# A convolutional recurrence on quarter arrays: the vertical pass of the second layer, with its transfers in pieces tied to its steps

## The reference, cut to what matters

```python
def _L1_conv_ref(x, down_w, down_b, right_w, right_b, left_w, left_b):
    def _conv1d(x, w, b):              # 5 taps, 48 channels to 48
        y = jax.lax.conv_general_dilated(x, w, window_strides=(1,), padding=[(2, 2)], ...)
        return y + b[None, :, None]
    def step(w, b):
        def f(carry, inp):
            nxt = inp + _conv1d(carry, w, b)
            return (nxt, nxt)
        return f
    xs = jnp.moveaxis(x, 2, 0)         # rows of the image
    _, d_rest = jax.lax.scan(step(down_w, down_b), d0, xs[1:])     # down
    _, u_rest = jax.lax.scan(step(down_w, down_b), u0, seq)        # and up again
    ...                                # then the same over columns, right and left
```

## Time and profile before

| | |
|---|---|
| median of 3 runs | 12709.53 us (12704.08 to 12710.47) |
| the profiled execution, its own time | 12698.42 us |
| its span | 12696.6 us |
| mean granted clock of TensorE | 0.985 |
| vertical stage, first to last matmul record | 2447.9 to 3774.7 us |
| horizontal stage, first to last matmul record | 3821.4 to 5151.8 us |

### The profile page before, as it was taken

The page is one execution under the profiler, slowest core; times in us unless marked ns, Lnnn a source line. Parts: engine busy times, 40 slices in busy tenths (PEclk is TensorE's granted clock), DMA queues, the critical chain, the costliest instruction groups (busy, mean ns, idle before and its releaser), DMA issues. The chain is left out here.

```text
span 12696.6 us, 315986 instructions
## 1 busy us (share of the span) xinstructions
PE 12256.2 (97%) x126170; PEld 8471.7 (67%) x126170; DVE 7918.9 (62%) x17482; ACT 5425.8 (43%) x11157; POOL 4647.4 (37%) x3557
## 2 busy tenths in 40 slices
PE   7999999899989999899999999999998999999999
PEld 6877434477767777555555555555556888888887
DVE  0000577533334544588888888888886777777777
ACT  0000111211213333455555555555555777777776
POOL 0000222100000045566666666666663444434444
PEclk9999999999999999899999999999999999999999
DMA  4333456783765488666666666666662222222222
GB/s 128 133 132 131 130 154 158 162 156 67 154 124 157 139 211 227 103 88 89 88 88 89 88 88 88 89 88 88 89 86 68 54 56 55 54 54 56 55 56 53
DMA packets 2310008, 1323.93 MB, mean 104 GB/s; under 512 B 1872228, under 2 KB 2219867, under 8 KB 2222959
## 3 DMA queue, kind: packets, MB, share of 16 engines
q1 hardware_dynamic: 2041484, 1201.47, 47.6%
q10 hardware_dynamic: 267232, 104.65, 3.5%
HBM read 648.72 MB, written 450.74 MB: 87 GB/s over the span
## 5 line engine op out<-in xcount | busy, mean ns | idle before, releaser
L1583 PE MATMUL l_m<-l_wa,l_pix 128*128 128x288 f32 x8192 | 2211.2, 413 | 14.0 <-DMA l_left<-k_rim_dram 14.0
L1583 PEld LDWEIGHTS l_m<-l_wa,l_pix 128*128 128x128 f32 x8192 | 1475.3, 190 | 699.9 <-issue 376.5
L1439 POOL TENSOR_TENSOR l_qkv<-l_qkv,l_copies 128x576 f32<-128x576 f32 x1024 | 1437.2, 1403 | 635.0 <-DVE l_qkv L1775 635.0
L1429 POOL TENSOR_TENSOR l_pix<-l_raw 128x516 f32<-128x516 f32 x1024 | 1216.3, 1188 | 1042.3 <-DVE l_t L1812 1017.0
L1285 PE MATMUL l1h_ps<-l1h_ring,l1h_w 96*96 96x256 f32 x6120 | 1327.2, 379 | 49.9 <-ACT l1h_ring L1233 46.3
L1056 PE MATMUL l1v_ps<-l1v_rows,l1v_w 96*96 96x256 f32 x6120 | 1326.1, 378 | 31.7 <-ACT l1v_rows L1029 31.7
L1285 PEld LDWEIGHTS l1h_ps<-l1h_ring,l1h_w 96*96 96x96 f32 x6120 | 999.0, 163 | 378.1 <-issue 46.7
L1269 POOL TENSOR_TENSOR l1h_columns<-l1h_blocks,l1h_ring 96x2048 f32<-96x2048 f32 x64 | 356.0, 5586 | 2418.6 <-DVE l1h_ring L1318 2418.6
L1056 PEld LDWEIGHTS l1v_ps<-l1v_rows,l1v_w 96*96 96x96 f32 x6120 | 990.5, 162 | 367.0 <-issue 30.8
L2093 PEld LDWEIGHTS l_e<-k_ident,l_turn 128*112 128x112 f32 x9900 | 1071.6, 133 | 204.4 <-issue 110.6
L2093 PE MATMUL l_e<-k_ident,l_turn 128*112 128x128 f32 x9900 | 1152.2, 274 | 51.5 <-DVE l_out L2256 46.8
(11 more groups left out here) (245 smaller groups left out, 21190.0 us busy)
## 6 DMA issues: line engine op xcount, KB each, us to landing
l0a_x<-x_px_dram SPq DMA_DIRECT2D x128, 1176.0 KB, 5.1
l0b_x<-x_in_dram SPq DMA_DIRECT2D x128, 493.8 KB
l_raw<-l_raw SPq DMA_DIRECT2D x128, 483.6 KB, 7.2
l_raw<-x_dram SPq DMA_DIRECT2D x1280, 48.0 KB, 3.7
l_x<-x3p_dram SPq DMA_DIRECT2D x132, 384.0 KB
l_out<-x_dram SPq DMA_DIRECT2D x528, 96.0 KB
out_dram<-l_out SPq DMA_DIRECT2D x132, 384.0 KB
x_dram<-l0b_out ACTq DMA_DIRECT2D x256, 193.5 KB, 3.1
```

The lines of the kernel that those rows point to most:

```text
L1429: nc.gpsimd.tensor_tensor(pix[:, n % 2, i, half * HALF:(half + 1) * HALF].rearrange("p (r w) -> p r w", w=PW), in0, in1, op).then_inc(pix_ ...
L1439: nc.gpsimd.tensor_tensor(q, q, copies[:, g % 2, 1:2, :].broadcast_to([128, 2, OUTC]), ALU.add)\
L1583: last = nc.tensor.matmul(bank[i][:, 0:OUTC], pix[:, k, i, first:first + 128], wa[:, b, i, :], start=True, stop=(i in (1, 2)))
```

## The change

The vertical stage alone gets another layout and another order of transfers; around it the stage ahead writes its rows in natural order, and the stage behind reads `up` by another stride.

A row now lies in one of two forms, in turn. Even rows are `whole`: partitions 0 to 47 hold one image of a group, 64 to 111 the other, all 256 columns with two zeros at each side. Odd rows are `parted`: partitions 0 to 47 hold the left 130 columns, 64 to 111 the right 130, both images side by side. A step takes a row of one form to a row of the other by 5 taps of four matmuls, one on each quarter of the array (`side(r)` picks the rows of the array, `side(c)` its columns), with 48 channels in and 48 out and 130 or 128 columns each. The sums of quarters in the two halves of rows go to two banks of PSUM. That is 20 matmuls for each step and group in the place of 3. DVE adds in one instruction over 112 partitions and 260 or 256 elements. Both buffers are cleared first (DVE and POOL), the first chunk is loaded ahead of the constants, half of the copies of parted rows are POOL's, and at the turn from down to up six copies on ACT and four on POOL bring the last row into both forms, for which PE waits (`kept`).

The transfers are the same bytes but for margins, in 8 pieces of some 400 KB for each batch. Going down, each piece of a save is issued behind one step of the first half of a chunk and each piece of a load behind one of the second half; going up, the stores have the first half and the loads back the second. A load from x or a store of a parted piece is two DMAs.

The diff, cut to its core:

```diff
-                                out_b[:, kk].rearrange("p n m (u q) -> p q n m u", q=2)[:, q],
-                                out[:, kk, :, 1 + q * HW2:1 + (q + 1) * HW2].rearrange("p m (n u) -> p n m u", n=WBLK),
+                                out_b[:, kk, q * (WBLK // 2):(q + 1) * (WBLK // 2)],
+                                out[:, kk, :, 1 + q * HW2:1 + (q + 1) * HW2].rearrange("p m (n w) -> p n m w", w=WB),
                                 ACT.Copy).then_inc(blocked, 1)
...
-                            place = out[:, kk, 2 * n:2 * n + 2, 1:W + 1].rearrange("p r (q u) -> p r u q", q=2)
+                            place = out[:, kk, 2 * n:2 * n + 2, 1:W + 1]
...
+        whole = sb("whole", [PP, SL, GI, RH, W + 2 * HALO])
+        parted = sb("parted", [PP, SL, GI, RH, 2, PART + 2 * HALO])
+        turn_w = sb("turn_w", [PP, 2, GI, WBLK, 2, RH, WB // 2])
+        turn_p = sb("turn_p", [PP, 2, GI, 2, WBLK // 2, 2, RH, WB // 2])
+        keep = sb("keep", [PP, GI, 2, PART])
+        w, bias = sb("w", [PP, TAPS, C]), sb("bias", [PP, 1])
+        gn_w, gn_p = sb("gn_w", [PP, GI, 2]), sb("gn_p", [PP, B, 2])
+        ps = [ctx.enter_context(nc.psum_tensor(f"l1v_ps{g}", [128, 2, 512], F32)) for g in range(2)]
...
+        def place(n):
+
+            return n if n <= LAST else 2 * LAST - n - 1
+
+        def source(n):
+
+            return n - 1 if n <= LAST else 2 * LAST - n
...
+            def load_x(c, pace):
...
+                    sp.wait_ge(saved[k], 128 * (c // SL))
                     for g in range(2):
-                        sp.wait_ge(product[g], (c - SL + 1) * CH)
+                        sp.wait_ge(product[g], 4 * (c - SL + 1) * CH)
+                else:
+                    sp.wait_ge(cleared_w, c + 1)
+                    sp.wait_ge(cleared_p, c + 1)
                 for i in range(B):
-                    for q in range(2):
-                        sp.dma_start(X[q * C:(q + 1) * C, k, i, :, 1:HW2 + 1],
-                                     D["x1"][i, :, c * CH + 1:(c + 1) * CH + 1, 1 + q * HW2:1 + (q + 1) * HW2])\
+                    rows = D["x1"][i, :, c * CH + 1:(c + 1) * CH + 1, :].rearrange("c (r t) w -> c t r w", t=2)
+                    pace(2 * i)
+                    sp.dma_start(whole[side(i % 2), k, i // 2, :, HALO:HALO + W], rows[:, 0, :, 1:W + 1])\
+                      .then_inc(loaded[k], 16)
+                    pace(2 * i + 1)
+                    for h in range(2):
+                        first = 1 + h * (W - PART)
+                        sp.dma_start(parted[side(h), k, i // 2, :, i % 2, HALO:HALO + PART], rows[:, 1, :, first:first + PART])\
                           .then_inc(loaded[k], 16)
...
+            def save_down(c, pace):
                 for g in range(2):
                     sp.wait_ge(state[g], c * CH + CH - 1)
+                for g in range(2):
+                    for h in range(2):
+                        for t, (here, there) in enumerate(both(c, g, h)):
+                            pace(4 * g + 2 * h + t)
+                            sp.dma_start(there, here).then_inc(saved[c % SL], 16)
...
+            def store_up(c, pace):
+                k = c % 2
+                sp.wait_ge(turned, 12 * (NCH - c))
+                sp.wait_ge(turned_low, 8 * (NCH - c))
                 for i in range(B):
-                    sp.dma_start(D["down"][i, :, c * CH:(c + 1) * CH, :], X[:, c % SL, i]).then_inc(saved[c % SL], 16)
...
+            def going_down(c, half):
+
+                return lambda m: sp.wait_ge(state[1], max(c * CH + half * RH + m, 1))
+
+            def going_up(c, half):
+
+                return lambda m: sp.wait_ge(state[1], up_step(c * CH + CH - 1 - half * RH - m))
+
+            def at_once(m):
+
+                pass
+            load_x(0, at_once)
+            sp.dma_start(w[:], D["l1_down"]).then_inc(consts, 16)
+            sp.dma_start(bias[:], D["l1_down_b"]).then_inc(consts, 16)
+            for h in range(2):
+                sp.dma_start(gn_w[side(h)], S["gn"][0:C, h:B:2, :]).then_inc(consts, 16)
+                sp.dma_start(gn_p[side(h)], S["gn"][0:C]).then_inc(consts, 16)
+            load_x(1, going_down(0, 0))
+            load_x(2, going_down(0, 1))
+            for c in range(1, NCH):
+                if c - 1 < NCH - SL:
+                    save_down(c - 1, going_down(c, 0))
+                if c + 2 < NCH:
+                    load_x(c + 2, going_down(c, 1))
+            for c in range(NCH - 2, -1, -1):
+                store_up(c + 1, going_up(c, 0))
+                if c + 1 >= SL:
+                    load_down(c + 1 - SL, going_up(c, 1))
+            store_up(0, at_once)
             for k in range(2):
-                sp.wait_ge(stored[k], 128 * (NCH // 2))
+                sp.wait_ge(stored[k], 192 * (NCH // 2))
...
             for c in range(NCH - 1, -1, -1):
                 if c < NCH - 2:
-                    act.wait_ge(stored[c % 2], 128 * ((NCH - 1 - c) // 2))
-                for i in range(B):
-                    if i % GI == 0:
...
+            for g in range(2):
+                pool.wait_ge(state[g], LAST)
+                for h in range(2):
+                    at = HALO + 2 * h
+                    nc.gpsimd.tensor_copy(whole[side(1 - h), SL - 1, g, RH - 1, HALO + h * HW2:HALO + (h + 1) * HW2],
+                                          parted[side(h), SL - 1, g, RH - 1, 1 - h, at:at + HW2]).then_inc(kept, 1)
+            for c in range(NCH - 1, -1, -1):
...
-            pe.wait_ge(consts, 64)
+            pe.wait_ge(consts, 96)
+            pe.wait_ge(blank, 2)
             for n in range(1, STEPS + 1):
-                before = n - 1 if n <= LAST else 2 * LAST + 1 - n
+                at = source(n)
+                k, row = at // CH % SL, at % CH // 2
                 for g in range(2):
                     if n == 1:
-                        pe.wait_ge(filled, (g + 1) * GI)
+                        pe.wait_ge(filled, 3 * g + 1)
+                    elif n == LAST + 1:
+                        pe.wait_ge(state[g], n - 1)
+                        pe.wait_ge(kept, 10)
                     else:
                         pe.wait_ge(state[g], n - 1)
-                    for s in range(3):
-                        last = nc.tensor.matmul(
-                            ps[g][0:C2, 0:GI * HW2], w[:, s, :],
-                            X[:, before // CH % SL, g * GI:(g + 1) * GI, before % CH, s:s + HW2],
-                            start=(s == 0), stop=(s == 2))
-                    last.then_inc(product[g], 1)
+                    for t in range(TAPS):
+                        for r in range(2):
+                            for c in range(2):
+                                if at % 2 == 0:
+                                    first = t + c * (W - PART)
+                                    x, width = whole[side(r), k, g, row, first:first + PART], PART
+                                else:
+                                    first = t + 2 * r
+                                    x, width = parted[side(r), k, g, row, c, first:first + HW2], HW2
+                                last = nc.tensor.matmul(ps[g][side(c), r, 0:width], w[side(r), t, :], x,
+                                                        start=(t == 0), stop=(t == TAPS - 1), skip_group_check=True)
+                                if t == TAPS - 1:
+                                    last.then_inc(product[g], 1)
...
+                    elif at < 0:
+                        dve.wait_ge(kept, 10)
+                    x = line(g, at)
+                    dve.wait_ge(product[g], 4 * n)
                     nc.vector.scalar_tensor_tensor(
-                        out=X[:, h // CH % SL, images, h % CH, 1:HW2 + 1],
-                        in0=ps[g][0:C2, 0:GI * HW2].rearrange("p (i u) -> p i u", i=GI), scalar=bias[:, 0:1],
+                        out=x, in0=ps[g][0:PP, :, 0:(HW2 if at >= 0 and at % 2 == 0 else PART)], scalar=bias[:, 0:1],
                         in1=x, op0=ALU.add, op1=ALU.add).then_inc(state[g], 1)
```

202 lines of the change are left out of this document (120 added, 82 removed).

## The result

The changed kernel takes **12921.76 us** (median of 4 runs, 12913.81 to 12927.6), the kernel before 12707.21 us on the same chip (12704.08 to 12710.47). The ratio is 1.0167, 95% interval 1.0155 to 1.0179: slower by 1.7%, where 0.9% faster was forecast.

The account below looks back on a forecast made before the run. PE was taken to bound the kernel, neither transfers nor DVE. From 12698.4 us, - 205 + 9 + 80 = - 116 gave 12582, and 11 us for the median 12593 us, 0.9% faster; range 12500 to 12760.

Parts of the forecast that it names:

- PE's work, less 205 us: Vertical stage: a group's matmuls on quarter arrays take 1.094 us in place of 1.295, over 1020 groups.
- The loop through DVE, nothing: Between steps of a group: drain, DVE's addition and signals take 0.84 us, covered by PE's 1.094 us on the other group.
- Start, turn and end, plus 9 us: Vertical stage's edges: plus 4 us for clearing and first loads, 2 at the turn, 3 for ACT's turning at the end.
- Transfers by themselves, nothing: SP's transfers in the vertical stage: same bytes, data a chunk ahead, scaled DMA share 0.84; no time added.
- so the pieces just fit: SP's stores: a piece holds SP 2.198 us, and a step would take 2.19 us.
- The instruction stream, plus 80 us: Vertical stage: 319 packets of 256 PE instructions, one each 3.50 us, some late behind data; stops sum to 79, taken as 80.
- Rival 2: Instruction packets nearly always late beyond the slack; break-even 0.61 us a packet, at 1.0 us net + 123: 12832 us; chance 0.13.
- The slack: Instruction packets: 2.5 us from a packet's start to running instructions leaves 1.0 us of 3.50 before lateness stops PE.
- The lateness: Packets behind loads: 2.3 us late, 1.3 us beyond the 1.0, halved to 0.65 us a packet.
- Which packets: Stops by half chunk: 75 packets behind loads at 0.65 us, 75 behind stores at 0.3, the other 169 at 0.05.
- thicker in ... first halves going up: Sign for the instruction term: PE's issue stops thicker in second halves of chunks going down and first halves going up.
- rival 1: Instruction fetching stays hidden, as in the setup stage, so that term is 0: - 196, 12513 us; chance 0.25.

Follow-up runs that it names:

- half_columns: Changed kernel with each matmul on only its first 65 (64) columns, same instruction count; recursion (first to last matmul of the vertical stage) 1488.2 us, changed kernel 1533.6.
- before_in_pieces: Kernel before with only its transfers changed, to pieces of 400 KB, each issued behind one step; ratio to before 1.0, recursion 1327.1 us.
- half_columns_eighth_bytes: Changed kernel with each matmul on half of its columns and transfers during the recursion cut to an eighth; recursion 1176.7 us.
- eighth_bytes: Changed kernel with each transfer issued during the recursion cut to one row in eight or one partition of 48; recursion 1200.5 us.
- batches: Changed kernel with 8 transfer pieces issued at once behind a batch's first step, not one behind each step; 13079.19 us, ratio to before 1.0294.
- finer: Changed kernel with each piece cut in two, 200 KB each, one behind each group's addition; 12798.59 us, ratio to before 1.0069, recursion 1432.5 us.
- finest: Changed kernel with each piece cut in four, 100 KB each, behind each group's last product and addition; 12718.93 us, ratio to before 1.0008, recursion 1328.8 us.
- fewer: Changed kernel with 3 matmuls for 5 on each quarter, same columns, 48 PE instructions a group and step for 80; 12607 us, recursion 1226.4 us.

## Why the prediction was wrong, by its steps

**PE's work, less 205 us: right.** A group takes 1.10 us where queues are idle; 1.094 was worked out from the last stage's fours. Without stops the recursion would be 1122 us, 205 less than before.

**The loop through DVE, nothing: right.** PE never waits for DVE in the changed kernel. Even at half of the columns only 21 us, PE and its loads taken together, are put down to DVE (half_columns).

**Start, turn and end, plus 9 us: right in sum, by luck.** The start takes 1.3 us more (4 forecast), the turn 1.8 (2), the end 6 (3); two errors cancel.

**Transfers by themselves, nothing: right for the data, wrong for SP.** before_in_pieces shows that their new order alone is worth nothing, and behind the first chunk PE waits for no ACT or DVE that is late for data. But "so the pieces just fit" failed: a parted piece of a store is two DMAs of 2.07 us each (median), in a step of 2.2 us, and the turned rows were not there at the half's start. What that does to the instruction packets is in the next term.

**The instruction stream, plus 80 us: this step failed.** The mechanism was the right one, its size off by a factor of five: 1533.6 - 1122 = 412 us, 1.29 us a packet in the place of 0.25. Rival 2 had 1.0, and the break-even was 0.61. Four readings were wrong:

1. *The slack.* "Of 3.50 us that leaves 1.0 us" took the 2.5 us from a packet's start to its first instruction for the whole cycle. As a reading it was good: behind the stops of the changed kernel it is 2.4 us in the median. But no row said that the next packet starts at once, and with nearly idle queues it starts 1.1 to 1.2 us behind the first record of the block before. The cycle is 3.69 us (half_columns_eighth_bytes), the slack 0.19 us below zero. With nearly idle queues 79 us are lost (eighth_bytes): all that I allowed for, before any packet is late. The setup stage, at 67 instructions a us without a stop, has a packet in 256 / 67 = 3.8 us, a little more than that cycle. It showed that 67 is possible, and nothing about 73.
2. *The lateness.* I took 2.3 us, less the 1.0, and halved the rest because "PE that stops also spreads the pieces". Without slack each us late stops PE. Measured, the data cost 333 us, 1.04 us over every packet, as rival 2 said it: "since a piece is always queued". That this is near rival 2's 1.0 is chance, as that was its example for all stops together.
3. *Which packets.* 0.65 us was put on loads of x, 0.3 on stores and 0.05 on "the other 169 packets". Measured, with the 0.25 that stays without data, a packet loses 1.6 us where x is loaded, 1.2 at stores, 0.9 at saves and 0.4 where nothing moves. Where the loads back are planned it loses 2.1 us, the most of all: 129 us in a place that the forecast held nearly free. The forecast's sign "thicker in ... first halves going up" is the wrong way round. In this half the end of the stores and two to four loads back are queued close together; in batches, with all of them at once, it loses 3.2 us. That points to the queue's depth, but no run spreads the loads back alone.
4. *The clock.* No term stood for it. It is 0.92 over the recursion, at most 111 of these 333 us (123 less the 12 at 0.99). It is much of what lies between stops of 0.7 us a packet and the loss of 1.0, and it goes as stops get short: 0.96 at 0.66 us idle a packet (finer), 0.99 at 0.41 (finest).

The rule of the Trainium skill that fetching is hidden, since instructions go out more slowly than blocks of them arrive (Runtime: NRT & Kernel Launch, Instruction fetch mechanics), was rival 1. The runs disagree with it where an engine wants more than 69 instructions a us, with idle queues too, and at 44 a us behind a DMA share of 0.83 (fewer, 69 us idle); in the kernel before, at 12,240 in 1326.8 us, 9 a us, they agree.

Rival 2, with a chance of 0.13, should have led. Its break-even of 0.61 us a packet lay beyond a slack of 1.0 us, and that reading kept it off.

## What to carry to other kernels

Count the instructions that a change adds, divide by the time that it is to take, and hold this rate against the fastest that any stage of the trace keeps up: here 69 a us was the end, and a plan at 73 lost 79 us with queues all but idle. Near this rate the DMA queues are on the engine's path, and the same bytes in pieces of 400, 200 and 100 KB cost 333, 232 and 128 us, until SP's 0.47 us for each issue ends it. When transfers are paced by steps, look on the issuing engine's timeline whether they are: here the way up fell out of step. A rate seen without a stop shows that it is possible, not that there is slack beyond it.

## What the runs showed of the hardware

- A packet of 256 PE instructions came every 3.69 us at best over a recursion, at a DMA share of 0.10 and with PE idle for 270 of 1177 us. Each of the 319 started behind the first record of the block before, and PE resumed 2.4 us behind a packet's start (median).
- Behind data a packet starts later: 1.6 to 2.2 us behind that record at a DMA share of 0.66 (changed), 1.1 to 1.2 at 0.10 (eighth_bytes).
- An issue of 50 KB holds SP 0.47 us, eight in 3.75 us, though a transfer of 400 KB of long rows needed no more than 0.3 to 0.6 us (390 KB saves of the changed kernel).
- The granted clock falls behind stops: 0.62 at 1.33 us idle a packet (half_columns, 423 of 1488 us), 0.86 at 1.10 (batches), 0.92 at 0.80 (changed), 0.99 at 0.41 (finest). Idle time a packet does not give it alone: half_columns_eighth_bytes has 0.80 at 0.85.
